# Layer 1's layer norm and transposes placed inside layer 0, the end of layer 0's last batch placed inside layer 1's scan

## The chip, the core and the metric

The kernel runs on one core of a Trainium2 chip. TensorE (PE) multiplies, VectorE (DVE), ScalarE (ACT) and GpSimd (POOL) do the element work, SyncE (SP) issues most DMAs. Every engine runs its own list of instructions strictly in the order in which the kernel writes it, and waits on semaphores for the others. The metric is device microseconds of one execution; the kernel before takes 2278.74 us (median of 3 runs, 2276.09 to 2279.93).

## The reference

Eight sequences (batches) of 512 tokens with 128 channels pass four layers; each layer is `xn = layernorm(x)`, then `x = x + attn(xn) + ffn(xn)`. The change concerns layers 0 and 1:

```python
# layer 0, attention: 16 heads of 8 channels with relative positions, then its own norm
ctx = softmax((q k^T + c2p + p2c) / scale) v
out = layernorm(ctx @ Wo + bo + xn, eps=1e-7) * ln_scale + ln_bias
# layer 0, ffn
ffn = xn @ sign(weight).T
# layer 1, attention: a minimal GRU in both directions, per channel, over the 512 tokens
z, h~ = sigmoid(xn @ Wz + bz), g(xn @ Wh + bh);  h[t] = (1 - z[t]) h[t-1] + z[t] h~[t]
out = concat(h_fwd, h_bwd) @ W_out + b_out
# layer 1, ffn: router xn @ w_router, the two best of 8 experts per token, 64 places per expert and
# sequence given out in order (a running count over tokens), experts with gelu, weighted sum back
```

Layers 2 (cross attention and a gated ffn) and 3 (channel attention and slots with 16 experts) are left as they were.

## The kernel before

X holds the tokens (32 tiles of 128 tokens by 128 channels, four tiles for a batch), XN the normed tokens and XT their transpose, all in SBUF. Each stage has one function per engine (`l0_pe`, `l0_dv`, ..., `l1_pe`, ...), and `after_l0` between them makes every engine wait for all of layer 0.

**Layer 0** is one pipeline of 512 steps, 64 for a batch: step u is one block of 128 queries of one head (16 heads times 4 blocks). In every step PE makes the scores, DVE adds the band (L181, form PS<-PS,AR) and takes the maximum (L193), ACT takes exp (L167) and copies the transposed probabilities (L171), POOL and the DMAs prepare the position terms two heads ahead. Small work of the neighbouring batches is put at fixed steps r of a batch, all of it through PSUM bank 7 (`B_M`), one use after another in the order of the list `order`. For the batch before these are `ENDS`: the last transposes of its heads (17), the transpose of the context (19), the output product `mo` (29), the ffn product `sw` (31), the square root on ACT (34), the norm on DVE (36, `tail(b, 2)`: a Newton step on 4 columns with `newton`, then four tensor_scalar of 128x128 by `ts`, L177), scale and sum on POOL (38), and statistics of the new X into NMV (48). The loop has 28 steps after the last (`STEPS0`), in which the last batch's end runs with nothing beside it. XN is in use there: it holds two of three buffers of the position terms (`CD`), the heads' output `OS` and the loaded scale, bias and output bias.

**Layer 1** begins with `after_l0`. Then SP issues 11 loads (L1082) and ACT two of 2 MB each (`wi`, `wo2`), and `norm_dv`, `norm_root`, `norm_po`, `norm_tr`, `norm_xt1` make XN and XT of all 32 tiles. PE then makes the 32 router products and starts the scan. The scan has 16 units, two directions for each batch. Unit u: two products of 128x512 on PE (`unit`), three sigmoids on ACT, `gate(u)` on DVE (L185), a multiplication on POOL, and on DVE the scan instruction of the unit before (`scan(u - 1)`, L1269). After the second unit of a batch PE makes the output products of the batch before (`scan_out`, 8 products of 128x128), and DVE adds them to X. DVE also runs the routing between units (`route(k)` after unit k: 0, 2, 3, 4 and 8); the running count over the tokens is 44 small products on PE (weights `trile` and `ones128`, 64 columns each), placed after unit 7. After the scan comes the dispatch: DVE builds one-hot tiles (DR), ACT and POOL split XN into a high and a low part (XH1 over XT, XL1), PE multiplies.

Of the kernel before, what the change touches and what calls it, by code (L numbers as in the profile page):

```python
# [13 lines left out]
SEQ = 512  # L14
# [204 lines left out]
def program(nc, a, out):  # L219
    ctx = ExitStack()  # L220
    with ctx:
# [13 lines left out]
        NMV = sb("NMV", [128, NT, 2])  # L235
        ar_at = -(-nc.sbuf_base // 32) * 32
        AR = sb("AR", [128, 40660])
# [133 lines left out]
        lst, lmv, ly, lv, ltmp = A0.take(4, 6), A0.take(4, 2), A0.take(4), A0.take(4), A0.take(4)  # L371
# [12 lines left out]
        ld_end = sem("ld_end")  # L384
# [10 lines left out]
        STEPS0 = 4 * NBH + 28  # L395
# [7 lines left out]
        ENDS = [{"heads": 17, "ct": 19, "mo": 29, "sw": 31, "root": 34, "norm": 36, "sum": 38, "last": 48}] * NB  # L403
        ENDS += [{"heads": 14, "ct": 16, "mo": 18, "sw": 19, "root": 21, "norm": 22, "sum": 23, "last": 25}]

        def small(u):
# [3 lines left out]
            if b >= 1 and r in (ENDS[b]["heads"], ENDS[b]["ct"], ENDS[b]["mo"], ENDS[b]["sw"]):  # L410
                uses += [(k, b - 1, 3 if k == "heads" else 0) for k in ("heads", "ct", "mo", "sw") if ENDS[b][k] == r]
# [6 lines left out]
        for u in range(STEPS0):  # L418
            order += small(u)
        number, emptied, n_ac, n_dv = {}, [], 0, 0  # L420
        for i, use in enumerate(order):
            number[use] = i
            if use[0] in ("q", "k", "far", "g0", "ct"):
# [13 lines left out]
        def l0_pe(pe):  # L437
# [13 lines left out]
            def small_mm(use):  # L451
# [124 lines left out]
            for u in range(STEPS0):  # L576
# [10 lines left out]
                if 0 <= G < 4 * NB and r in (0, 2, 4, 6):  # L587
                    pv(G, r // 2)


        def l0_dv(dv):
# [100 lines left out]
            def tail(b, k):  # L692
                ps, xs = quarters(PS[:, B_M, :]), slice(b * 4, b * 4 + 4)
                if k == 0:
                    dv.wait_ge(m_mm, number["mo", b, 0] + 1)
                    dv.wait_ge(ld_end, 3 * 16)
                    tt(dv, T1, ps, bc(bot.unsqueeze(1), [128, 4, 128]), ALU.add).then_inc(m_dv, 1)
                elif k == 1:
# [6 lines left out]
                    ts(dv, lv, lmv[:, :, 1], 1e-7, None, ALU.add).then_inc(tn_v, 1)  # L705
                elif k == 2:
                    dv.wait_ge(tn_v, b + 1)
                    dv.wait_ge(tn_q, b + 1)
                    dv.step(newton(dv, ly, lv, ltmp))
# [3 lines left out]
                    ins.then_inc(tn_n, 1)  # L713
                else:
# [7 lines left out]
            for u in range(STEPS0 + 1):  # L722
# [8 lines left out]
                if b >= 1:  # L731
                    at = ENDS[b]
                    if r == at["heads"] + 1:
                        heads_out(b - 1, 3)
                    if r == at["mo"] + 1:
                        tail(b - 1, 0)
                    if r == at["sw"] + 1:
                        tail(b - 1, 1)
                    if r == at["norm"]:
# [1833 lines left out]
```

## Time and profile before

| | us |
|---|---|
| median of 3 runs | 2278.74 (2276.09 to 2279.93) |
| the profiled execution's own time | 2277.15 |
| its span | 2275.3 |
| layer 0's products end | about 929 |
| last batch's end, on all engines | 929 to 945 |
| layer 1's norm and transposes | 945 to 962 |
| router products | 962 to 975 |
| scan with routing | 975 to 1047 |

Busy over the whole span: PE 85%, DVE 78%, ACT 63%, POOL 54%. That mean says little here: in layer 0 PE and DVE are near their limits together, while between 929 and 1047 us one engine after another waits for a chain. The profiled execution's own time is 1.85 us more than its span, and the median is 1.6 us more than the profiled execution.

### The profile page before, as it was taken

The numbers are of one execution on the slowest core, as the hardware profiler recorded it, in microseconds if no ns is written. First come the engines' busy times: TensorE is split into PE (matmuls) and PEld (weight loads), VectorE is DVE, ScalarE is ACT, GpSimd is POOL, SyncE is SP. The second block draws the span as 40 slices with busy tenths as digits, with TensorE's granted clock in tenths as the row PEclk, the third lists the DMA queues.
The fourth block names the chain that finished last, engine by engine and source line by source line (L and its number), as shares of the span: only waits on it lengthen the run. The fifth ranks groups of instructions, "written<-read, shape, count | busy, mean of one in ns | idle before, by whom it ended". The sixth has DMA issues, their size and how long they took to land.

```text
span 2275.3 us, 38965 instructions
## 1 busy us (share of the span) xinstructions
PE 1944.4 (85%) x13526; PEld 1473.7 (65%) x13526; DVE 1763.7 (78%) x4099; ACT 1430.5 (63%) x2795; POOL 1223.2 (54%) x1028
## 2 busy tenths in 40 slices
PE   3799898888989898587996999999998468788898
PEld 2566565666666666464683878777876345566797
DVE  7688888888888888457187888888887699873586
ACT  2578777777878777344235666666665257765575
POOL 3777677777777775148053445444543466426400
PEclk9999999999999999789997999999999689999999
DMA  3988788888878786201000000000001000003000
GB/s 105 306 304 303 249 294 274 288 268 278 284 271 281 278 300 227 85 1 35 3 6 1 1 1 1 1 1 1 1 1 31 0 0 1 1 1 98 24 2 38
DMA packets 73877, 264.15 MB, mean 116 GB/s; under 512 B 12273, under 2 KB 32241, under 8 KB 73169
## 3 DMA queue, kind: packets, MB, share of 16 engines
q1 hardware_dynamic: 72304, 254.31, 33.2%
q10 hardware_dynamic: 1376, 7.34, 0.8%
q8 instruction: 109, 1.79, 0.3%
q14 instruction: 88, 0.71, 0.1%
HBM read 140.30 MB, written 121.31 MB: 115 GB/s over the span
## 4 chain that ended last, share of the span: by engine, by line
PE 38%; DVE 8%; ACT 6%; POOL 2%; issue 2%; DMA 0%; POOLq 0%; ACTq 0%; DVEq 0%; SPq 0%
PE PS L157 10%; PE PS L161 7%; PE PS L163 7%; PE PS L162 7%; PE PS L326 7%; ACT AR L167 3%; ACT L167 2%; DVE AR L181 1%; DVE DR L181 1%; DVE PT L181 1%; ACT AR L171 1%; ACT PT L171 1%; DVE AR L185 1%; DVE AR L200 1%; DVE AR L193 1%
## 5 line engine op out<-in xcount | busy, mean ns | idle before, releaser
L167 ACT ACTIVATE AR<-PS,AR 128x512 f32<-128x512 f32 x1008 | 686.6, 688 | 286.8 <-DVE AR L193 178.8
L193 DVE TENSOR_REDUCE AR<-PS 128x1 f32<-128x512 f32 x896 | 616.4, 688 | 119.3 <-PE PS L163 100.5
L326 PE MATMUL PS<-ident,AR 128*128 128x128 f32 x3816 | 584.6, 277 | 86.1 <-ACT AR L171 38.6
L157 PE MATMUL PS<-AR 128*9 128x512 f32 (+8 forms) x4190 | 503.5, 360 | 93.0 <-DVE AR L181 32.9
L326 PEld LDWEIGHTS PS<-ident,AR 128*128 128x128 f32 x3816 | 435.0, 142 | 200.6 <-issue 71.2
L181 POOL TENSOR_TENSOR AR<-AR 128x512 f32<-128x512 f32 (+6 forms) x310 | 380.6, 1244 | 226.9 <-DVE AR L181 97.0
L157 PEld LDWEIGHTS PS<-AR 128*9 128x9 f32 (+5 forms) x4190 | 288.8, 133 | 298.4 <-DVE AR L181 130.1
L171 ACT ACTIVATE AR<-PS 128x512 f32<-128x512 f32 (+3 forms) x612 | 356.4, 587 | 91.8 <-PE PS L326 47.7
L176 POOL TENSOR_SCALAR AR<-AR 128x512 f32<-128x512 f32 x144 | 245.4, 1704 | 293.2 <-DVE AR L1596 219.4
L171 ACT ACTIVATE PT<-PS 128x512 fp32r<-128x512 f32 x320 | 191.5, 599 | 208.3 <-PE PS L326 171.5
L181 DVE TENSOR_TENSOR PS<-PS,AR 128x192 f32<-128x192 f32 (+1 forms) x512 | 201.7, 394 | 118.0 <-PE PS L534 112.0
L181 DVE TENSOR_TENSOR AR<-PS,AR 128x512 f32<-128x512 f32 (+3 forms) x321 | 210.0, 655 | 40.8 <-PE PS L157 36.2
L181 POOL TENSOR_TENSOR AR<-XN,AR 128x192 f32<-128x192 f32 (+1 forms) x170 | 201.5, 1206 | 60.9 <-DMA XN<-scr 42.9
L181 DVE TENSOR_TENSOR PT<-PS,PT 128x512 fp32r<-128x512 f32 x320 | 217.7, 680 | 5.0 <-ACT PT L171 5.0
L181 POOL TENSOR_TENSOR AR<-AR,XN 128x512 f32<-128x512 f32 x144 | 154.3, 1074 | 104.4 <-DVE AR L181 74.8
L534 PE MATMUL PS<-AR 128*128 128x320 bf16 (+3 forms) x1024 | 197.3, 275 | 0.0
L531 PE MATMUL PS<-ident,XN 128*128 128x128 f32 x680 | 131.1, 275 | 0.0
L161 PE MATMUL PS<-MH,XNr 128*128 128x512 f32 x256 | 123.5, 483 | 5.2 <-ACT AR L167 2.8
L176 DVE TENSOR_SCALAR AR<-AR 128x512 f32<-128x512 f32 (+6 forms) x229 | 113.9, 501 | 1.3
L534 PEld LDWEIGHTS PS<-AR 128*128 128x128 bf16 x1024 | 101.1, 99 | 6.2
L163 PE MATMUL PS<-MH,XNr 128*128 128x512 f32 x256 | 102.1, 399 | 0.0
L161 PE MATMUL PS<-PT,VW 128*128 128x512 f32 x256 | 101.5, 396 | 0.0
(157 smaller groups left out, 3001.9 us busy)
## 6 DMA issues: line engine op xcount, KB each, us to landing
scr<-AR SPq DMA_DIRECT2D x128, 800.0 KB, 4.3
XN<-scr SPq DMA_DIRECT2D x85, 768.0 KB, 6.6
AR<-scr SPq DMA_DIRECT2D x43, 768.0 KB, 6.5
AR<-qsc SPq DMA_DIRECT2D x96, 192.0 KB
qsc<-AR SPq DMA_DIRECT2D x96, 128.0 KB, 3.4
AR<-in_wgu SPq DMA_DIRECT2D x16, 256.0 KB, 3.2
X<-in_x ACTq DMA_DIRECT2D x1, 2048.0 KB, 8.5
AR<-in_wi ACTq DMA_DIRECT2D x1, 2048.0 KB, 8.2
```

The lines of the kernel that those rows point to most:

```text
L157: return pe.e.matmul(out, lhsT, rhs, start=start, stop=stop)
L161: pe.e.matmul(out, l[0], r[0], start=start, stop=False)
L162: pe.e.matmul(out, l[1], r[0], start=False, stop=False)
L163: return pe.e.matmul(out, l[0], r[1], start=False, stop=stop)
L167: return ac.e.activation(out, in_, func, bias=bias, scale=scale, accum_out=accum)
L171: return ac.e.activation(out, in_, ACT.Copy, bias=0.0, scale=1.0)
L176: return en.e.tensor_scalar(out, in0, s1, None, op0)
L181: return en.e.tensor_tensor(out, in0, in1, op)
L193: return dv.e.tensor_reduce(out, in_, AX.X, ALU.max, negate=True)
L326: return pe.e.transpose(out, in_, ident[0:k, 0:k])
L531: pe.e.matmul(out, lhsT, rhs, start=start, stop=start, is_transpose=True, skip_group_check=True)
L534: return pe.e.matmul(out, lhsT, rhs, start=False, stop=stop, skip_group_check=True)
```

## The change

**Layer 0.** In batches 2 to 7 of the pipeline, the norm at step 36 (`tail(b, 2)`, b from 1 to 6) also norms the tokens of batch b - 1 for layer 1. Its Newton step takes 8 columns instead of 4; a copy stores the scale in NY, and four more tensor_scalar of 128x128 write the normed tokens to XR, a buffer that otherwise holds the splits of q and k. At step 45 PE transposes XR (4 products) into bank 7, and at step 46 ACT copies them to XT. So the first six batches are transposed before layer 0 ends. `STEPS0` goes from 28 extra steps to 14, without the last batch's end.

**Layer 1.** Each engine begins the scan once `pv_mm` says that layer 0's last products are made. SP's 11 loads wait for that too; the two 2 MB loads come from SP now, after `after_l0`, and lie where nothing of layer 0 is needed. `END0` puts the last batch's end between the units of the scan: heads 0, ct 1, mo 2, sw 3, root 4, norm 5, sum and xt (batch 6's transposes) 6, last 7, and the last batch's own norm for layer 1 at root7 8, norm7 9, tr7 10. DVE writes the normed tokens of batch u into XN after unit u (`normed`, units 0 to 6). The router products are cut into eight groups of four (`ROUTER`). The routing moves to units 13, 14 and 15 with its last part after the scan, and the running count (`trail`) from after unit 7 to after unit 15's products. Exp and the normalization of the router's probabilities come after the scan.

VectorE at step 36 of a batch in layer 0, before (AR is the working area, T1 in it; the last row is the next batch's v with its bias):

```order
L208 RECIPROCAL AR<-AR 128x4 [waits l0_tn_q,l0_tn_v]
L181 TENSOR_TENSOR AR<-AR 128x4 [waits own_dv] x2
L177 TENSOR_SCALAR AR<-AR 128x4 [waits own_dv]
L181 TENSOR_TENSOR AR<-AR 128x4 [waits own_dv]
L177 TENSOR_SCALAR AR<-AR 128x128 [waits own_dv]
L177 TENSOR_SCALAR AR<-AR 128x128 x3
L181 TENSOR_TENSOR AR<-PS,AR 128x64x8 [waits l0_pv,l0_m_mm]
```

The same place of the changed kernel:

```order
L208 RECIPROCAL AR<-AR 128x8 [waits l0_tn_q,l0_tn_v]
L181 TENSOR_TENSOR AR<-AR 128x8 [waits own_dv] x2
L177 TENSOR_SCALAR AR<-AR 128x8 [waits own_dv]
L181 TENSOR_TENSOR AR<-AR 128x8 [waits own_dv]
L177 TENSOR_SCALAR AR<-AR 128x128 [waits own_dv]
L177 TENSOR_SCALAR AR<-AR 128x128 x3
L730 COPY NY<-AR 128x4 [waits l0_sp_a,l0_sp_p]
L177 TENSOR_SCALAR AR<-X,NMV,AR 128x128 x4
L181 TENSOR_TENSOR AR<-PS,AR 128x64x8 [waits l0_pv,l0_m_mm]
```

A copy and four tensor_scalar stand between the norm and what the pipeline does next.

VectorE in the scan, two units of the kernel before with nothing between them (L185 is a gate, L1269 a scan, the row with X the output of a batch):

```order
L185 SCALAR_TENSOR_TENSOR AR<-PS,AR 128x512 [waits l1_sig,l1_u_mm]
L1269 SCALAR_TENSOR_TENSOR AR<-AR 128x512 [waits l1_gz_po]
L185 SCALAR_TENSOR_TENSOR AR<-PS,AR 128x512 [waits l1_sig,l1_u_mm]
L1269 SCALAR_TENSOR_TENSOR AR<-AR 128x512 [waits l1_gz_po]
L181 TENSOR_TENSOR X<-X,PS 128x512 [waits l1_bout,l1_so_mm]
```

Unit 5 of the changed kernel (its scan is L1335):

```order
L185 SCALAR_TENSOR_TENSOR AR<-PS,AR 128x512 [waits l1_sig,l1_u_mm]
L1335 SCALAR_TENSOR_TENSOR AR<-AR 128x512 [waits l1_gz_po]
L181 TENSOR_TENSOR X<-X,PS 128x512 [waits l1_bout,l1_so_mm]
L177 TENSOR_SCALAR XN<-X,NMV,NY 128x128 x4
L208 RECIPROCAL AR<-AR 128x8 [waits l0_tn_q,l0_tn_v]
L181 TENSOR_TENSOR AR<-AR 128x8 [waits own_dv] x2
L177 TENSOR_SCALAR AR<-AR 128x8 [waits own_dv]
L181 TENSOR_TENSOR AR<-AR 128x8 [waits own_dv]
L177 TENSOR_SCALAR AR<-AR 128x128 [waits own_dv]
L177 TENSOR_SCALAR AR<-AR 128x128 x3
L730 COPY NY<-AR 128x4
L177 TENSOR_SCALAR AR<-X,NMV,AR 128x128 x4
```

Twelve tensor_scalar of 128x128 and a Newton step stand in one unit here; other units carry less.

TensorE at the end of the scan of the changed kernel, from unit 15's products on (`l1_rt_dv` is the routing's semaphore; 128x8x8 are the 64 columns of the running count, and DR the dispatch):

```order
L157 MATMUL PS<-XT,AR 128x512 [waits l1_sig]
L157 MATMUL PS<-XT,AR 128x512 [waits l1_g_dv]
L157 MATMUL PS<-AR 128x128 [waits l1_so_dv,l1_scan]
L157 MATMUL PS<-AR 128x128 x7
L157 MATMUL PS<-AR 128x8x8 [waits l1_ones,l1_rt_dv]
L157 MATMUL PS<-AR 128x8x8 x35
L157 MATMUL PS<-AR 128x128 [waits l1_so_dv,l1_scan]
L157 MATMUL PS<-AR 128x128 x7
```

The eight rows have the same forms as those after unit 7 before, where units 8 to 15 still follow; here the last output products and the dispatch follow.

The diff, cut to its core:

```diff
-        STEPS0 = 4 * NBH + 28
+        STEPS0 = 4 * NBH + 14
-        ENDS = [{"heads": 17, ..., "last": 48}] * NB
-        ENDS += [{"heads": 14, "ct": 16, "mo": 18, "sw": 19, "root": 21, "norm": 22, "sum": 23, "last": 25}]
+        ENDS = {"heads": 17, "ct": 19, "mo": 29, "sw": 31, "root": 34, "norm": 36, "sum": 38, "xt": 45, "last": 48}
+            if 2 <= b < NB and r == ENDS["xt"]:
+                uses.append(("xt", b - 2, 0))
...
+                elif what == "xt":
+                    pe.wait_ge(tn_n, 2 * b + 3)
+                    for q in range(4):
+                        ins = tr(pe, ps[:, q * 128:q * 128 + 128], XR[:, q * 128:q * 128 + 128])
...
+                    w = 8 if b else 4
+                    dv.step(newton(dv, ly[:, 0:w], lv[:, 0:w], ltmp[:, 0:w]))
...
+                    if b:
+                        done = 6 * min(b + 3, NB)
+                        dv.wait_ge(sp_p, done)
+                        dv.wait_ge(sp_a, done)
+                        dv.step(dv.e.tensor_copy(NY[:, 4 * b - 4:4 * b], ly[:, 4:8]))
+                        for i in range(4 * b - 4, 4 * b):
+                            ins = ts(dv, XR[:, i % 4 * 128:i % 4 * 128 + 128], X[:, i, :], NMV[:, i, 0:1], ly[:, 4 + i % 4:5 + i % 4],
+                                     ALU.subtract, ALU.mult)
+                        ins.then_inc(tn_n, 1)
...
+            def xt_out(b):
+                ac.wait_ge(m_mm, number["xt", b, 0] + 1)
+                copy(ac, XT[:, b * SEQ:b * SEQ + SEQ], PS[:, B_M, :]).then_inc(m_ac, 1)
...
+        END0 = {"heads": 0, "ct": 1, "mo": 2, "sw": 3, "root": 4, "norm": 5, "sum": 6, "xt": 6, "last": 7, "root7": 8, "norm7": 9,
+                "tr7": 10}
+        ROUTER = {1: (0, 4), 2: (4, 8), 3: (8, 12), 4: (12, 16), 5: (16, 20), 7: (20, 24), 9: (24, 28), 12: (28, 32)}
         def l1_sp(sp):
+            sp.wait_ge(pv_mm, 4 * NB)
...
+            after_l0(sp)
+            for dst, name in ((wi, "wi"), (wo2, "wo2")):
+                sp.e.dma_start(dst, a[name]).then_inc(ld[1], 16)
...
+            for u in range(16):
+                unit(u)
+                for what, b, g in (("heads", LAST, 3), ("ct", LAST, 0), ("mo", LAST, 0), ("sw", LAST, 0), ("xt", LAST - 1, 0)):
+                    if u == END0[what]:
+                        small_mm((what, b, g))
+                if u in ROUTER:
+                    for i in range(*ROUTER[u]):
+                        ins = mm(pe, PS[:, 6, i * 8:i * 8 + 8], XT[:, i * 128:i * 128 + 128], router, True, True)
...
+                if u % 2 and u >= 3:
+                    scan_out(u // 2 - 1)
+                if u == END0["tr7"]:
+                    pe.wait_ge(xn_dv, NB)
...
+            pe.wait_ge(m_ac, n_ac + 1)
+            trail()
             scan_out(NB - 1)
+            after_l0(pe)
...
+            ROUTE = {13: (0,), 14: (3,), 15: (4,)}
             for u in range(16):
                 gate(u)
                 if u:
                     scan(u - 1)
                 if u % 2 and u >= 3:
                     scan_out(u // 2 - 1)
-                route(u)
+                for k in ROUTE.get(u, ()):
+                    route(k)
+                if u < LAST:
+                    normed(u)
...
             scan(15)
+            route(8)
             scan_out(7)
+            after_l0(dv)
```

## Rows read from the trace of the kernel before

**Rows 1.** Busy time by stage: start:end, length, then each engine's (count), TensorE clock, DMA share, GB/s.

```profile
170.00:830.00 660.00, 588.64 (x5157) 418.95 (x5156) 560.73 (x1206) 505.12 (x894) 494.68 (x447) 1.00 0.83 280
928.80:945.40 16.60, 4.49 (x32) 3.67 (x32) 5.39 (x23) 2.68 (x4) 3.78 (x3) 0.76 0.00 0
945.40:961.80 16.40, 7.88 (x33) 6.33 (x33) 12.78 (x64) 5.19 (x12) 4.91 (x6) 0.50 0.76 291
961.80:975.40 13.60, 13.60 (x64) 13.60 (x65) 0.00 (x0) 0.00 (x0) 0.00 (x0) 0.50 0.00 0
975.40:1047.30 71.90, 56.84 (x265) 36.71 (x265) 50.08 (x62) 34.75 (x60) 46.01 (x31) 0.93 0.00 1
```

**Rows 2.** Timeline at the boundary: start, length, engine, line, form, count.

```profile
925.16 3.62 PE L157 MATMUL PS<-AR 128*9 128x512 f32 x32 [0.69 <-ACT AR L171]
1004.16 9.99 PE L157 MATMUL PS<-AR 128*128 128x64 f32 x88
1047.26 6.71 DVE L181 TENSOR_TENSOR DR<-AR 128x512 fp32r<-128x512 f32 x11
```

**Rows 3.** Chain of waits through one pair of units of the scan.

```profile
1025.77 2.93 PE PS L157 x18
1028.72 0.90 ACT AR L167 x2
1030.67 0.75 DVE AR L185
1031.42 1.14 DVE AR L1269
```

**Rows 4.** Timeline of ACT: when layer 0's output OS (in XN) is copied, every 16 steps.

```profile
119.66 0.60 ACT L171 ACTIVATE XN<-PS 128x512 f32<-128x512 f32 x1
143.83 0.60 ACT L171 ACTIVATE XN<-PS 128x512 f32<-128x512 f32 x1
435.20 0.60 ACT L171 ACTIVATE XN<-PS 128x512 f32<-128x512 f32 x1
467.38 0.60 ACT L171 ACTIVATE XN<-PS 128x512 f32<-128x512 f32 x1
```

**Rows 5.** Timeline of DVE and POOL at step 36 of a batch in layer 0.

```profile
450.84 2.36 POOL L181 TENSOR_TENSOR AR<-XN,AR 128x192 f32<-128x192 f32 x2 [0.58 <-DVE PS L181]
...
451.54 1.88 DVE L181 TENSOR_TENSOR AR<-AR 128x4 f32<-128x4 f32 x2
...
453.85 1.12 DVE L177 TENSOR_SCALAR AR<-AR 128x128 f32<-128x128 f32 x4
454.88 0.69 DVE L181 TENSOR_TENSOR AR<-PS,AR 128x512 f32<-128x512 f32 x1
```

**Rows 6.** Timeline of SP's queue: the first and the twelfth load at the kernel's start.

```profile
0.72 0.39 SPq L2479 DMA_DIRECT2D ident<-in_ident  x1
6.82 0.45 SPq L2484 DMA_DIRECT2D AR<-in_l_sw  x1
```

**Rows 7.** DMA issues by line at the start: count, KB, us to landing.

```profile
ident<-in_ident SPq DMA_DIRECT2D x1, 96.0 KB, 2.2
```

**Rows 8.** Timeline of ACT at the start of the scan.

```profile
977.57 1.28 ACT L167 ACT_TABLE_LOAD   x1 [15.95 <-PE PS L157]
978.87 3.58 ACT L167 ACTIVATE AR<-PS,AR 128x512 f32<-128x512 f32 x6
```

**Rows 9.** Timeline of DVE: the routing's second choice between two units.

```profile
998.70 1.43 DVE L185 SCALAR_TENSOR_TENSOR AR<-AR 128x256 f32<-128x256 f32 x1
1001.98 0.42 DVE L181 TENSOR_TENSOR AR<-AR 128x256 f32<-128x256 f32 x1
```

**Rows 10.** Busy time in stretches of 2 us around a fall and a rise of the clock.

```profile
986.00:988.00 2.00, 0.00 (x0) 0.00 (x0) 0.56 (x1) 2.00 (x5) 1.30 (x2) 1.00 0.00 0
988.00:990.00 2.00, 0.62 (x3) 0.63 (x4) 1.97 (x4) 1.07 (x2) 1.73 (x1) 0.65 0.00 0
994.00:996.00 2.00, 2.00 (x5) 0.77 (x4) 1.86 (x5) 1.10 (x2) 0.75 (x1) 0.64 0.00 0
```

More of the change, by code:

```diff
@@ L744, in l0_dv @@
                     heads_out(b, HEADS.index(r - 1))
-                if b >= 1 and r == ENDS[b]["last"]:
+                if 1 <= b < NB and r == ENDS["last"]:
                     tail(b - 1, 3)
+            return heads_out, tail
         def l0_ac(ac):
@@ L927, in l0_po @@
                     split(b + 1, k // 2, k % 2)
-                if b >= 1 and r == ENDS[b]["sum"]:
+                if 1 <= b < NB and r == ENDS["sum"]:
                     tail(b - 1)
+            return tail
         def l0_sp(sp):
@@ L1057, in program @@
         H_ = [A1.take(512) for _ in range(4)]
+        assert A1.top <= PTN * 2048
+        wi, wo2 = A1.take(8, 512), A1.take(8, 4, 128)
         XIN = A1.take(8, 8, 64)
@@ L1276, in scan_out, with normed @@
                 tt(dv, X[:, xs, :], X[:, xs, :], quarters(PS[:, 4 + b % 2, :]), ALU.add).then_inc(so_dv, 1)
+            def normed(b):
+                dv.settle()
+                for i in range(4 * b, 4 * b + 4):
+                    ins = ts(dv, XN[:, i, :], X[:, i, :], NMV[:, i, 0:1], NY[:, i:i + 1], ALU.subtract, ALU.mult)
+                ins.then_inc(xn_dv, 1)
+            ROUTE = {13: (0,), 14: (3,), 15: (4,)}
             for u in range(16):
@@ L1283, in l1_dv @@
                     scan_out(u // 2 - 1)
-                route(u)
+                for k in ROUTE.get(u, ()):
+                    route(k)
+                if u < LAST:
+                    normed(u)
+                if u == END0["heads"]:
+                    heads_out(LAST, 3)
+                if u == END0["mo"]:
+                    tail(LAST, 0)
+                if u == END0["sw"]:
+                    tail(LAST, 1)
+                if u == END0["norm"]:
+                    tail(LAST, 2)
+                if u == END0["last"]:
+                    tail(LAST, 3)
+                    dv.settle()
+                    ts(dv, v7, NMV[:, 4 * LAST:NT, 1], 1e-5, None, ALU.add).then_inc(tn_v, 1)
+                if u == END0["norm7"]:
+                    dv.wait_ge(tn_v, NB + 1)
+                    dv.wait_ge(tn_q, NB + 1)
+                    dv.step(newton(dv, NY[:, 4 * LAST:NT], v7, tmp7))
+                    dv.settle()
+                    normed(LAST)
             scan(15)
+            route(8)
             scan_out(7)
+            after_l0(dv)
             dv.wait_ge(rt_dv, 3)
@@ L1293, in l1_dv @@
                    ALU.is_equal).then_inc(d_dv, 1)
+            dv.wait_ge(a_ac, 49)
+            dv.step(red(dv, s8, PROB, ALU.add))
+            dv.settle()
+            dv.step(dv.e.reciprocal(s8, s8))
+            dv.settle()
+            tt(dv, PROB, PROB, col(s8), ALU.mult).then_inc(rt_dv, 1)
             for p in range(4):
@@ L2485, in run_sp @@
             l0_sp(sp)
-            after_l0(sp)
             l1_sp(sp)
```

234 lines of the change are left out of this document (123 added, 111 removed).

## The prediction

> **What bounds the kernel now.** I read the page first: TensorE 85%, VectorE 78%, and a low stretch in slices 16 to 18. The busy time by stage says what that is [rows 1]. In layer 0, 660 us of its middle hold 588.6 us of PE and 560.7 us of DVE work, 89% and 85%: two engines near their limit that also wait for each other. From 928.8 us on nothing is near a limit: 16.6 us for the last batch's end (DVE 5.4 us busy, PE 4.5), 16.4 us for layer 1's norm, 13.6 us in which only PE works, at a granted clock of 0.50, and 71.9 us of scan with DVE at 50.1 us. Then I read the timeline at the boundary [rows 2]: layer 0's last products end at 925.16 + 3.62 = 928.8 and the dispatch begins at 1047.3 with DVE's first DR tile. These 118.5 us are what the change rewrites. Last the chain of waits in the scan [rows 3]: output products and the next unit's first product 2.93, two sigmoids 0.90, a third one until 1030.67, gate 0.75, scan 1.14, and again; a pair of units takes 1032.6 - 1025.8 = 6.8 us, and DVE is free for about 1.3 us of it.
>
> **Layer 0, what is added.** Six times, at step 36, DVE gets a copy, a small tensor_scalar and four tensor_scalar of 128x128. Four of these take 454.88 - 453.85 = 1.03 us to the next instruction [rows 5]; for the two small ones I add 0.3, which makes 1.35 us. At step 45 PE gets four transposes, about 0.5, and ACT a copy of 0.6 like those of rows 4. Is it hidden? The same place tells: the 16 steps after step 28 take 143.83 - 119.66 = 24.2 us in batch 0, which has no batch before it, and 467.38 - 435.20 = 32.2 us in batch 3, which has the products, statistics, square root and norm of the batch before [rows 4]. So 8.0 us are paid for some 6 us of DVE work, 3 of PE and 3 of ACT: nothing of DVE's part is hidden, and a bit more than DVE's part is paid, since PE and DVE wait for each other in turn. For the new work I take 2.2 us a batch: 1.35 of DVE, 0.5 of PE, and 0.35 for bank 7, which is now used at 45 and again at 47. Six batches: +13.2 us. The lower end is DVE's alone with a fifth of it absorbed, 1.1 us a batch or 6.6; a gain is excluded, since nothing is taken from these steps. The upper end takes the ratio 8.0 to 6 on all of it with the whole bank handover, 3.0 a batch or 18.
>
> **Layer 1, from the end of layer 0's products (0) to the first DR tile.** Removed: the 16.6 us of the last batch's end, the 16.4 of the norm and the 13.6 of the router as stretches of their own.
>
> *Start.* SP's 11 loads are issued only at 0. Twelve went out from 0.72 to 6.82, 0.55 apart, and the first landed 2.2 after its issue [rows 6, 7]: ten distances and a landing are 7.7 us. PE is idle for them, and the clock will be low, since an idle PE from before 986 to 989 lost it by 990 [rows 10]. A product of 0.90 then takes 1.8, then table load 1.28, three sigmoids 1.8 (six took 3.58 [rows 8]): first gate at 12.6. Before, the tail of layer 0 ran in this time; now nothing does.
>
> *The scan is now DVE's.* Its 50.1 us stay, without 1.3 for the probabilities that move behind the dispatch's start. Added: the last batch's end 5.4 [rows 1], eight batches normed into XN at 1.03 with a small wait, 8.8, batch 6's XR and copy 1.2, statistics of the last batch 1.3, its Newton step 1.2. That makes 66.7, of which 4.0 (last scan, last part of the routing, last output) come after the running count: 62.7. To it come DVE's remaining waits, for which I walked through the units in the order of the code with these durations: 1.7 in units 0 and 1 (chain as in rows 3); 1.5 for the first output products behind `mo`, `sw` and router products on PE; 0.8 at unit 4 for the square root between two table loads; 3.0 at unit 7, because PE's transposes of batch 6 wait for DVE's norm at unit 5 and unit 7's products stand behind them; 2.2 at unit 9 for the second square root's table loads; 1.5 at unit 11 behind the last batch's transposes; 2.8 in the bare pairs 10 to 13. Together 13.5. The second choice of the routing ends at 12.6 + 62.7 + 13.5 = 88.8.
>
> The router's products, 64 records of 0.21 at half clock in 13.6 us, are some 0.9 a group at full clock and fall into time in which PE waits for DVE: 0. The 2 MB loads need no one before the expert products: 0. The probabilities' sum, reciprocal and product stand on DVE where it waits for expert products: 0; POOL's first weights, now behind them, have that slack too.
>
> *The running count.* 88 records took 9.99 us at full clock in the middle of PE work [rows 2]. Now they stand behind unit 15, and DVE makes the second choice just before: a gate, a scan, an output and 1001.98 + 0.42 - 998.70 = 3.7 us of choice [rows 9], while PE has only one batch's output products (2.0). PE is idle for some 6 us, longer than before the fall at 988 to 990 [rows 10]. At 0.50 the count begins at 0.21 us a record as the router's did. The clock came back by 995 after some 5 us of output products and unit products [rows 10], and did not come back in 13.6 us of router products [rows 1]. The count has 64 columns where these have 128, 512 and 8. I take a rise after 5 us: 23 records in 5 us, 65 in 7.4, 12.4 in all. Ends: 10.0 and 19.
>
> *End.* After the count output products 2.0 and DVE's addition 0.7: first DR at 88.8 + 12.4 + 2.7 = 103.9 instead of 118.5, that is -14.6.
>
> **Sum.** -14.6 + 13.2 = -1.4. The profiled execution took 2277.15 (span 2275.3, 1.85 around it), so 2275.8; the median lies 1.6 above it: 2277.4, rounded to 2277.5.
>
> The Trainium skill bears on two terms. POOL's two band products occupy 450.84 to 453.2, and DVE's two products on 4 columns, begun at 451.54, take 1.88 us [rows 5]: they end when POOL does. "SBUF — State Buffer" (engine ports, the shared port pair) calls it an exclusive lock between a GpSimd operation and a DVE operation with two SBUF inputs or in a two-port mode. By it the moved choice would be slowed by POOL's multiplications, as 3.7 us for five short instructions already shows, and the tensor_scalar only in a two-port mode; with 0.5 us for half of the 48 new ones the sum would be some 12 us worse, an estimate, and a rival below has that mechanism. "ScalarE: Activation LUTs" (What ACT_TABLE_LOAD costs) gives 1.28 us and a drain of 1.38 for each switch. The trace agrees with the first and shows 0.02 us from the load's end to the next sigmoid [rows 8]. By the page four added loads would be 5.5 us dearer, by the rows nothing.
>
> **The rivals.**
> - *Layer 0 hides half* (faster). DVE has 15% free and PE 11% in the mean [rows 1]; if the pipeline catches up behind step 36, layer 0 costs 6.6 instead of 13.2, and with a count at full clock (-2.4): -10.4, so 2268.5. Against it: 8.0 us paid for the same kind of work [rows 4].
> - *The count at half clock* (slower). The place is behind unit 15. If 64 columns count as little as the router's 8, 88 records take 19 and the output products behind them 2 more: +8.6, total +7.2, 2286. It decides once DVE's work keeps PE idle so long that the clock falls before the count and the count does not raise it again; with a clock that stays, the count costs 10.
> - *DVE held by POOL* (slower). In the scan DVE's load no longer leaves the 1.3 us a pair in which collisions vanished. If half of the 16 scans and 32 tensor_scalar lose 0.5 us each, that is +12: 2289. For it: 1.88 us for two products of 4 columns [rows 5]; against it: four tensor_scalar took no more than 1.12.
>
> **How the numbers follow.** This kernel's measurement can tell about 0.2%, 4.6 us, from no change. The forecast, a change between -4.6 and +4.6, has 0.38; the hidden half and its milder forms 0.33; the count at half clock 0.19; POOL's lock, or full cost in layer 0 with a half-clock count, 0.10. Faster 0.33, same 0.38, slower 0.29. Layer 0 leaves -6.6 to +5, the count -2.4 to +8.6, the scan's waits 4 either way; they seldom fall together, so 2265 to 2290 holds 8 in 10. The likeliest case's own range is 2273 to 2283.
>
> **What would show it.** In the changed profile: the distance of OS copies from step 28 to 44 should be 34 to 35 us in batches 2 to 7 (32.2 before), and layer 0's products should end at 939 to 945. First gate 12 to 13 us after them. DVE busy at least 0.7 of the scan. Running count 88 records in 12 to 19 us, with a clock near 0.5 at its start; first DR some 104 us after layer 0's products. The prediction is wrong if OS copies stay at 32.2, if PE does not lose its clock before the count, or if the stretch takes more than 112 us.

## The result

The changed kernel takes 2286.44 us (median of 7 runs, 2283.89 to 2288.79) against 2278.74 for the kernel before (median of 7 runs in the same session, 2276.09 to 2284.00): ratio 1.0032, 95% interval 1.0020 to 1.0043. The same kernel measured again, in 11 runs, gave 2286.78 and 1.0030 (1.0020 to 1.0040); its profile is called the second one below. The forecast was 2277.5, a change of -1.4; it is slower by 7 to 8 us. The profiled execution took 2286.73 with a span of 2284.9.

Where it went is read at the boundary of layers 0 and 1. First the timeline of PE and DVE in the changed kernel, answering [rows 2]: start, length, engine, line, operation, form, count, and in brackets the idle time before and what ended it.

```profile
940.89 3.62 PE L157 MATMUL PS<-AR 128*9 128x512 f32 x32 [0.69 <-ACT AR L171]
951.05 3.78 PE L157 MATMUL PS<-XT,AR 128*128 128x512 f32 x4 [6.53 <-DMA AR<-in_rev]
1035.26 19.14 PE L157 MATMUL PS<-AR 128*128 128x64 f32 x88 [6.80 <-DVE AR L181]
...
956.49 0.75 DVE L185 SCALAR_TENSOR_TENSOR AR<-PS,AR 128x512 f32<-128x512 f32 x1 [5.13 <-PE PS L157]
...
1055.04 6.71 DVE L181 TENSOR_TENSOR DR<-AR 128x512 fp32r<-128x512 f32 x11
```

Layer 0's products end at 940.89 + 3.62 = 944.5, 15.7 us later than before. The first gate follows 12.0 us behind, and the running count begins 90.75 us behind. It has 72 of the 88 records, two for each of its 36 products; the other 16 records are the last 8 output products, and the 44 products given for the count in the section on the kernel before are both together. The dispatch begins 1055.04 - 944.51 = 110.5 us behind layer 0's products, where it was 118.5. So: +15.7 in layer 0, -8.0 in layer 1. In the second profile layer 0's products end at 942.0 and the dispatch begins 111.0 us behind them: +13.2 and -7.4. From the first DR tile to the end of the span it is 1228.0 us before, 1229.9 after and 1228.1 in the second profile: behind the boundary no change is clear of what profiles of one kernel differ by.

Second, busy time of the three stages of layer 1, answering [rows 1]: start:end, length, each engine's busy time (count), granted TensorE clock, DMA share, GB/s.

```profile
944.50:956.50 12.00, 5.47 (x14) 2.74 (x12) 0.34 (x5) 3.77 (x6) 0.20 (x1) 0.72 0.18 47
956.50:1035.30 78.80, 54.22 (x271) 36.05 (x269) 68.33 (x127) 38.33 (x64) 48.69 (x31) 0.93 0.13 54
1035.30:1055.00 19.70, 19.10 (x88) 18.80 (x88) 3.33 (x6) 0.00 (x0) 2.78 (x5) 0.52 0.00 0
```

The last row is the news: 19.7 us in which PE does nearly all the work, at half clock. In steps of 4 us around it (same columns):

```profile
1028.00:1032.00 4.00, 0.46 (x5) 0.26 (x3) 3.93 (x7) 1.28 (x7) 2.19 (x2) 1.00 0.00 2
1032.00:1036.00 4.00, 0.74 (x4) 0.75 (x4) 3.83 (x7) 0.00 (x0) 4.00 (x6) 0.72 0.00 0
1036.00:1040.00 4.00, 4.00 (x20) 4.00 (x20) 0.60 (x1) 0.00 (x0) 2.08 (x4) 0.50 0.00 0
...
1048.00:1052.00 4.00, 4.00 (x20) 4.00 (x20) 1.05 (x3) 0.00 (x0) 0.00 (x0) 0.50 0.00 0
1052.00:1056.00 4.00, 2.42 (x13) 2.16 (x11) 1.99 (x5) 0.00 (x0) 0.00 (x0) 0.72 0.00 0
```

PE is nearly idle from 1028 to 1035, the clock falls from 2.4 to 1.2 GHz in the second row, and it stays at 0.50 through some 16 us of unbroken work of 64-column products. It is back only in the last row, near the end of the output products (128 columns), which begin at about 1051.

Layer 0 shows as forecast in the copies of OS on ACT [rows 4]:

```profile
435.68 0.60 ACT L171 ACTIVATE XN<-PS 128x512 f32<-128x512 f32 x1
469.06 0.60 ACT L171 ACTIVATE XN<-PS 128x512 f32<-128x512 f32 x1
```

33.4 us in this batch (34.6 in the second profile), 35.0 and 34.3 in the two behind it, against 32.2 before; the 16 steps behind, which hold the new transposes, take 25.5 instead of 24.7.

### The profile page after: what moved, and what is told of

Same layout as the page of the kernel before. It is cut to its first block, busy times and chain, and to the rows that moved or that the text cites. A ratio compares the mean times of both kernels' runs of the same rounds, so it can differ in the third digit from the quotient of the medians.

```text
span 2284.9 us, 39010 instructions
## 1 busy us (share of the span) xinstructions
PE 1947.4 (85%) x13526; PEld 1478.5 (65%) x13526; DVE 1776.3 (78%) x4127; ACT 1431.9 (63%) x2794; POOL 1222.8 (54%) x1024
## 3 DMA queue, kind: packets, MB, share of 16 engines
q10 hardware_dynamic: 1088, 3.15, 0.4%
## 4 chain that ended last, share of the span: by engine, by line
PE 61%; DVE 20%; ACT 9%; issue 5%; POOL 3%; DMA 2%; SPq 0%; POOLq 0%; ACTq 0%; DVEq 0%
PE PS L157 19%; PE PS L326 14%; PE PS L161 7%; PE PS L163 7%; PE PS L162 7%; DVE AR L181 4%; ACT AR L167 4%; DVE AR L193 3%; PE PS L541 3%; PE PS L538 3%; ACT AR L171 2%; POOL AR L181 2%; DVE XN L177 2%; ACT L167 2%; DVE PS L181 2%
## 5 line engine op out<-in xcount | busy, mean ns | idle before, releaser
L157 PE MATMUL PS<-AR 128*9 128x512 f32 (+8 forms) x4190 | 514.7, 365 | 97.3 <-DVE AR L181 47.7
L326 PEld LDWEIGHTS PS<-ident,AR 128*128 128x128 f32 x3844 | 440.7, 142 | 206.3 <-issue 82.5
L157 PEld LDWEIGHTS PS<-AR 128*9 128x9 f32 (+5 forms) x4190 | 298.2, 136 | 301.5 <-DVE AR L181 146.1
L162 PE MATMUL PS<-MH,XL 128*128 128x512 f32 x256 | 102.2, 399 | 0.0
```

The costliest lines, as they stand in the source:

```text
L157: return pe.e.matmul(out, lhsT, rhs, start=start, stop=stop)
L162: pe.e.matmul(out, l[1], r[0], start=False, stop=False)
L326: return pe.e.transpose(out, in_, ident[0:k, 0:k])
```

## The experiments

**What makes the count slow.** Theory A: PE stands idle for DVE's second choice, the clock falls, and the narrow count cannot raise it. First, the idle time was filled with work that nothing needs.

```diff
             pe.wait_ge(m_ac, n_ac + 1)
+            pe.wait_ge(ld[1], NL1 + 32)
+            for k in range(7):
+                mm(pe, PS[:, 7, :], w1[k % 4], wi[:, k, :], True, True)
             trail()
```

> The changed kernel with seven 128x512 products on weights already loaded put in front of the running count, into the bank that the count then overwrites; PE thus works through the 6.8 us in which it waited for the second choice. Theory A (the count is slow because PE stood idle before it and the clock fell to 0.50): granted clock 1.00 in the count, the group of 88 records takes 10 us instead of 19.1, first DR tile about 9 us earlier, total 2277 to 2279. Rival B (the group is slow for its waits or for its 64-column products whatever stood before): the clock is 0.50 again or the group stays at 17 to 19 us, total 2285 to 2288. Rival C (the count is faster but something else releases the dispatch): group at 10 us, first DR less than 4 us earlier, total above 2282.

Measured: 2275.44 us (12 runs), ratio to before 0.9988 (0.9980 to 0.9996). The group in the timeline of its profile, and the clock while it ran:

```profile
1034.38 10.09 PE L157 MATMUL PS<-AR 128*128 128x64 f32 x88 [0.80 <-DVE AR L181]
```

```profile
1036.00:1040.00 4.00, 4.00 (x38) 4.00 (x38) 0.00 (x0) 0.00 (x0) 1.21 (x3) 1.00 0.00 0
```

The same 88 records take 10.09 us at 2.4 GHz instead of 19.14 at 1.2; the dispatch begins 103.4 us behind layer 0's products instead of 110.5. Theory A stands: useless work of 6 us makes the kernel 11 us faster by the medians, 10 by the ratios to the kernel before. 7 to 8 us of them are seen at this place. Single profiles can't be held to the microsecond: in seven profiles of kernels with the same layer 0 its products end between 939.4 and 946.0.

**Is it the idle alone, or the narrow products too?** The same filling with 28 products of 64 columns:

```diff
-            for k in range(7):
-                mm(pe, PS[:, 7, :], w1[k % 4], wi[:, k, :], True, True)
+            for k in range(28):
+                mm(pe, PS[:, 7, 0:64], w1[k % 4], wi[:, k % 8, 0:64], True, True)
```

> The changed kernel with 28 products of 64 columns in front of the running count in place of the seven of 512 columns of the filled kernel; at full clock they take about as long (28 x 0.22 = 6.2 us). Theory A1 (what keeps TensorE's clock is that it works at all): clock 1.00 in the count, 88 records in 10 us, total 2275 to 2278 as with wide filling. Theory A2 (narrow products do not hold or raise the clock, as the 72 records of the count and the router's did not raise it): clock 0.50 in the count, filling itself slower (up to 12 us), 88 records in 19 us, total 2286 to 2293. In both the records of the filling alone tell it.

Measured: 2284.73 us, ratio 1.0039 (1.0025 to 1.0053). Its count, and its PE in stretches around the count's start:

```profile
1036.62 16.60 PE L157 MATMUL PS<-AR 128*128 128x64 f32 x88 [0.62 <-DVE AR L181]
```

```profile
1032.00:1036.00 4.00, 3.99 (x36) 3.85 (x35) 3.86 (x7) 0.00 (x0) 4.00 (x5) 1.00 0.01 2
1036.00:1040.00 4.00, 3.38 (x24) 3.39 (x25) 1.92 (x3) 0.00 (x0) 3.45 (x6) 0.82 0.01 4
1038.00:1039.00 1.00, 1.00 (x10) 1.00 (x9) 0.00 (x0) 0.00 (x0) 1.00 (x4) 0.80 0.06 16
1040.00:1044.00 4.00, 4.00 (x21) 4.00 (x21) 0.00 (x0) 0.00 (x0) 0.00 (x0) 0.50 0.00 0
```

The filling itself ran at full clock, which A2 had not said, and so did the first 2 us of the count. Then the clock fell, at 1038 to 1039, in a stretch in which PE was busy all the time. So neither theory holds as it was written: in these runs the narrow products did not bring the clock back (some 16 us in the changed kernel, 13.6 in the router before), and here they did not keep it either. The 9.99 us of the count in the kernel before passed at 1.00 with 128x512 products right ahead of it, as in the kernel with the wide filling.

**Does the late place do it by itself?** The kernel before, with nothing but its routing steps moved to units 14 and 15 and the count behind unit 15:

```diff
-                if b == 3:
+                if b == 7:
+                    scan_out(b - 1)
                     pe.wait_ge(rt_dv, 2)
...
-                route(u)
+                route({3: 1, 4: 1, 8: 1, 14: 3, 15: 4}.get(u, u))
             scan(15)
+            route(8)
             scan_out(7)
```

> The kernel before with nothing but its first and second choice moved from units 3 and 4 to units 14 and 15 of the scan and the running count from behind unit 7 to behind unit 15 and the output products of batch 6. Theory A (the late place alone brings the idle and the half clock): PE waits some 6 us for the second choice, the group of 88 records takes 18 to 19 us at a granted clock of 0.50; against before the stretch loses the whole group of 10 us from the scan's middle only where PE was the limit there, so total 9 to 15 us above before, 2288 to 2294. Rival (the half clock comes from the changed kernel's own scan, in which PE idles for DVE's added work): the clock stays at 1.00 and the total is 3 to 6 us above before.

Measured: 2291.25 us, ratio 1.0056 (1.0038 to 1.0073), that is +11.6.

```profile
1044.50 19.14 PE L157 MATMUL PS<-AR 128*128 128x64 f32 x88 [6.41 <-DVE AR L181]
```

The same 19.14 us, with 6.41 of idle ahead. The clock in the count was 0.50 here too. The loss needs nothing of the changed kernel's DVE load; it belongs to the place.

**Choice one unit earlier.**

```diff
-        ROUTER = {1: (0, 4), 2: (4, 8), 3: (8, 12), 4: (12, 16), 5: (16, 20), 7: (20, 24), 9: (24, 28), 12: (28, 32)}
+        ROUTER = {1: (0, 4), 2: (4, 8), 3: (8, 12), 4: (12, 16), 5: (16, 20), 7: (20, 24), 9: (24, 28), 11: (28, 32)}
...
-            ROUTE = {13: (0,), 14: (3,), 15: (4,)}
+            ROUTE = {12: (0,), 13: (3,), 14: (4,)}
```

> The changed kernel with the last router group at unit 11 instead of 12 and the three routing steps on DVE at units 12, 13, 14 instead of 13, 14, 15: when PE is through with unit 15 the second choice should be there. Theory A: the count begins without a long idle at a clock of 1.00, takes 10 us, and lies beside DVE's gate 15, scans and output addition; 9 us for the clock and up to 4 for the overlap, less what PE waits for at unit 11 (the copy of the last tokens): first DR 8 to 12 us earlier, total 2274 to 2279. Rival B (small-column products are slow by themselves): the count still takes 15 us, gain only from the overlap, 3 to 4 us, total 2282 to 2284. Rival D (the last tokens arrive too late at unit 11, PE waits there and the clock falls there): no gain, 2285 to 2289.

Measured: 2280.84 us, with single runs from 2271.15 to 2286.86; ratio 1.0001 (0.9986 to 1.0017). Inconclusive as a median; its profile, of a run of 2284.44, shows one way in which it fails:

```profile
1030.14 2.84 PE L157 MATMUL PS<-AR 128*128 128x128 f32 x16 [3.15 <-DVE AR L1335]
1033.78 18.62 PE L157 MATMUL PS<-AR 128*128 128x64 f32 x88 [0.80 <-DVE AR L181]
```

```profile
1024.00:1028.00 4.00, 2.99 (x7) 0.97 (x6) 3.86 (x7) 3.54 (x6) 3.09 (x2) 1.00 0.00 0
1028.00:1032.00 4.00, 1.86 (x13) 1.86 (x14) 3.93 (x6) 3.33 (x11) 2.12 (x1) 0.90 0.00 0
1032.00:1036.00 4.00, 3.20 (x16) 2.90 (x15) 3.90 (x7) 0.00 (x0) 1.54 (x1) 0.50 0.01 2
```

The wait right before the count is gone (0.80), but 3.15 us of idle one group earlier cost the clock as well, and the narrow count kept it low. With the clock kept it should be some 9 us less, and the runs at 2271 to 2273 would fit that. It is not shown: no profile of such a run was taken, and the kernel before spreads as widely, over 9.7 to 16.1 us in the four sets of its runs beside the experiments.

**The count in wider products.** 12 products of 64 to 256 columns instead of 36 of 64; the idle before stays.

```diff
-                    for q in range(4):
-                        prev = [(v, j) for j in range(q)] + ([(v1, j) for j in range(4)] if k else [])
-                        ins = mm(pe, ov[:, :, q, :], trile, v[:, :, q, :], True, not prev)
-                        for x, (pv_, j) in enumerate(prev):
-                            ins = mm(pe, ov[:, :, q, :], ones128, pv_[:, :, j, :], False, x == len(prev) - 1)
+                    mm(pe, ov, trile, v, True, False)
+                    prev = [(v, j, j + 1) for j in range(3)] + ([(v1, j, 0) for j in range(4)] if k else [])
+                    for x, (pv_, j, q0) in enumerate(prev):
+                        ins = mm(pe, ov[:, :, q0:4, :], ones128, bc(pv_[:, :, j:j + 1, :], [128, 8, 4 - q0, 8]), False, x == len(prev) - 1)
```

> The changed kernel with the same count written in 12 products of 64 to 256 columns instead of 36 of 64 columns (a product with the triangle over all four tiles of a batch, the earlier tiles' ones repeated in the moving operand); the 6.8 us idle before it stay. The columns stay 2304. By 0.45 us a record of 512 columns at full clock and 0.9 at half: 4.1 us at full, 8.1 at half, against 7.9 and 15.3 of the narrow form. Theory A3 (wider products raise the clock again): some 5 to 6 us and the output products behind at full clock, first DR 11 to 12 us earlier, total 2274 to 2276. Theory A4 (half clock throughout): 8.1 + 3.8 us, first DR 7 us earlier, total 2279 to 2280.

Measured: 2273.67 us, ratio 0.9987 (0.9977 to 0.9998).

```profile
1034.26 8.55 PE L157 MATMUL PS<-AR 128*128 128x256 f32 x40 [6.80 <-DVE AR L181]
```

```profile
1036.00:1038.00 2.00, 2.00 (x9) 1.82 (x8) 0.00 (x0) 0.00 (x0) 1.08 (x3) 0.50 0.00 0
1038.00:1040.00 2.00, 2.00 (x11) 1.90 (x10) 0.00 (x0) 0.00 (x0) 0.00 (x0) 0.72 0.00 0
1040.00:1042.00 2.00, 2.00 (x16) 1.90 (x15) 0.91 (x3) 0.00 (x0) 0.00 (x0) 1.00 0.00 0
```

Theory A3: after the same 6.80 us of idle the clock is back some 5 us into the group, as the forecast had it, only with wide products; 8.55 us in place of 19.14 for the count and the output products. The wide form has a third of the products for the same 2304 columns. Whether their width or their number matters to the clock, these runs do not separate.

**Layer 0's additions.** All of them left out for batches 0 to 5 (layer 1 then works on stale tokens), and only the transposes and copies left out (cut; the second change of the diff is in the first kernel alone, and in both the waits of other engines for what is gone are moved):

```diff
-            if 2 <= b < NB and r == ENDS["xt"]:
-                uses.append(("xt", b - 2, 0))
...
-                    if b:
+                    if b and b < NB - 1:
+                        dv.step(dv.e.tensor_copy(NY[:, 4 * b - 4:4 * b], ly[:, 4:8]))
+                    elif b:
```

> The changed kernel without what it adds to layer 0's pipeline in batches 0 to 5: the four 128x128 tensor_scalar at step 36, the four transposes and the copy at step 45. Layer 1 then works on stale tokens there; the reciprocal roots, the root with twice the width and layer 1's own order stay. Theory A (the additions cost 3.2 us a batch): layer 0's products end 19 us earlier, near 925, total 2267 +- 2. Rival E (2.2 us a batch as forecast, the rest of the later end comes from something else): 13 us, total 2273 +- 2. Rival F (only DVE's part counts): 8 us, total 2278.

> As the kernel without layer 0's additions, but with the four tensor_scalar a batch back in; left out are the transposes on PE and the copies on ACT for batches 0 to 5 (layer 1 works on stale tokens there). Theory A (DVE's part is paid in full and PE's and ACT's too): 6 x 1.35 = 8 us above the kernel without any, 11 us below the changed kernel: about 2275. Rival F (only DVE's part counts): equal to the changed kernel, 2286. Rival G (DVE has slack and only bank 7's handover counts): equal to the kernel without any, 2267.

Measured: 2272.24 us without any (ratio to before 0.9970, 0.9959 to 0.9981), 2281.38 with the tensor_scalar alone (1.0005, 0.9997 to 1.0014). From the changed kernel's 2286.4 to 2286.8 that makes 14.2 to 14.5 us for the whole, 9.1 for the tensor_scalar, 5.1 to 5.4 for the rest. The ends of layer 0's products, first without any, then with the tensor_scalar:

```profile
923.86 3.62 PE L157 MATMUL PS<-AR 128*9 128x512 f32 x32 [0.69 <-ACT AR L171]
```

```profile
931.27 3.62 PE L157 MATMUL PS<-AR 128*9 128x512 f32 x32 [0.69 <-ACT AR L171]
```

These ends, 927.5 and 934.9, are 17.0 and 9.6 us ahead of the changed kernel's 944.5, or 14.5 and 7.1 ahead of the second profile's 942.0. So the whole is 14 to 17 us, and the split is less certain than the medians make it look: 7.4 for the tensor_scalar by these two rows. The medians are lower because both kernels lose some 3 us again in layer 1. Their scan, from first gate to count, takes 82.2 us where it takes 78.8 and 79.6 in the changed kernel, at the same DVE work but a lower clock (row of the kernel without any); why the clock falls earlier there is open.

```profile
939.50:1021.70 82.20, 57.55 (x269) 38.81 (x268) 68.32 (x127) 38.27 (x64) 48.66 (x31) 0.88 0.13 52
```

In batch 3 the 32 steps from step 28 take 57.1 us without any, 58.1 with the tensor_scalar, 58.9 and 60.1 in the two profiles of the changed kernel: 1.9 to 3.0 us a batch where the forecast had 2.2. My expectation of 19 us for the whole (2267 in all) was too high, and the second kernel's 2281.38 lies between its theory A (2275) and rival F (2286); rival E (13 us, 2273) held, and the forecast's 13.2 (8.1 + 5.1) was nearly right.

**The norm in the scan.** Three of four tensor_scalar left out in seven batches (stale tokens in the dispatch):

```diff
-                for i in range(4 * b, 4 * b + 4):
+                for i in range(4 * b, 4 * b + 4 if b == LAST else 4 * b + 1):
```

> The changed kernel with three of the four tensor_scalar left out that write each of the first seven batches' normed tokens into XN in the scan (the dispatch then gets stale tokens for these). Step of the forecast: 8.8 us for eight batches at 1.03 each with a small wait. If DVE is the limit all through the scan and POOL's multiplications do not hold these instructions up: 7 x 0.77 = 5.4 us less. Theory P (they wait for POOL, as 2.0 to 5.1 us for a batch in the profile instead of 1.1 say): 8 to 12 us less where the held-up time goes with them. Rival (the held-up time only moves to the next DVE instruction, or PE and ACT take over as the limit): 3 to 5 us less. Total 2274 to 2283 in all, first gate to count 78.9 us in the changed kernel as it is.

Measured: 2279.65 us, ratio 1.0001 (0.9989 to 1.0013), 7 us less. Its scan from first gate to count:

```profile
951.30:1028.40 77.10, 56.36 (x271) 38.19 (x269) 58.49 (x106) 38.27 (x64) 48.63 (x31) 0.89 0.14 55
```

and the waits of DVE in that stretch, first of the changed kernel, then of this one (what waited, for what, us in total, times, longest):

```profile
DVE AR L185 <- ACT AR L167: 7.4, 4, 2.6
```

```profile
DVE AR L185 <- ACT AR L167: 19.9, 11, 5.1
```

DVE loses 9.8 us of work for 21 instructions, 0.47 each where a free one takes 0.28 [rows 5], and the stretch loses 1.7 (78.8 to 77.1; 2.5 against the changed kernel's second profile): the gates then wait for the sigmoids. The second row above also holds the first gate's wait of 5.1, which lies ahead of the stretch and which the first row lacks; without it the gates wait 14.8 us instead of 7.4, 7.4 more. The scan is not DVE's alone; PE, ACT, DVE and POOL take turns in it, and most of the work taken away was replaced by waits. How much of that is the clock's doing is open: PE's clock in the stretch was 0.89 here, 0.93 and 0.90 in the two profiles of the changed kernel. The medians differ by 7 us, more than the scan shows. In this profile layer 0, where nothing was edited, ends 2.5 to 5.1 us earlier than in the two of the changed kernel; where the rest of the 7 us lies stays open. The changed kernel, run once more to see whether its first median had been an accident:

> The changed kernel once more, unedited, beside the kernel before. The run without three quarters of the scan's norm work took 7 us less than the changed kernel by the medians, but its profile shows the scan only 1.7 us shorter and the rest of the difference in layer 0, where nothing was edited. If the changed kernel's first figure was right: 2285 to 2288 again, ratio 1.003. If part of the 7 us is how layer 0 happened to run: 2281 to 2284, ratio 1.001 to 1.002.

Measured: 2286.78 us, ratio 1.0030 (1.0020 to 1.0040). It had not.

**Loads earlier.** Layer 1's weights placed in buffers of layer 0's probabilities that are free one group of heads earlier:

```diff
-            sp.wait_ge(pv_mm, 4 * NB)
+            sp.wait_ge(pv_mm, 4 * NB - 1)
+        A1.top = 2 * 2048
         w1 = [A1.take(128) for _ in names1]
...
+        w1_end, A1.top = A1.top, 0
```

> The changed kernel with layer 1's weights and constants put where probabilities of layer 0 lie that are free one group of heads earlier, so that their 11 loads go out some 25 us before layer 0's products end. Expected: PE's wait of 6.5 us for the last load goes; first unit's products start 1 us after layer 0's products instead of 6.5, at full clock (0.9 us a product instead of 1.8): first gate 5 us after layer 0's products instead of 12.0, total 7 us less, 2279 to 2280. Rival (DVE or the head's end becomes the wait: the last head's reciprocal and product come first): first gate 8 to 9, total 2282 to 2283.

Measured: 2278.22 us, ratio 0.9999 (0.9983 to 1.0015): 8.2 to 8.6 less than the changed kernel. PE's next product follows without a wait, and DVE's first gate comes 4.4 us behind layer 0's products (939.72 + 3.62) instead of 12.0:

```profile
943.27 1.99 PE L157 MATMUL PS<-XT,AR 128*128 128x512 f32 x4
...
947.77 0.75 DVE L185 SCALAR_TENSOR_TENSOR AR<-PS,AR 128x512 f32<-128x512 f32 x1 [3.96 <-ACT AR L167]
```

Of these 7.6 us 5.9 to 6.5 reach the dispatch, which begins 104.6 us behind layer 0's products; the scan takes 80.8 us here, at a clock of 0.86.

**All together.** Early choice, wide count, early loads, with and without three wide products of filling at unit 15:

> The changed kernel with the choice one unit earlier, the wide count, the early loads and three 128x512 products as filling before the output products of unit 15. If the three gains add up (7 for the loads, 10 for the clock, up to 4 for the count beside DVE's last scans and 3.8 for the wide count): total 2262 to 2266, 13 to 17 us below the kernel before. If the count hides wholly behind DVE's gate 15, scans and output addition, the last terms overlap and it is 2265 to 2269. Rival (clock falls once in a while in the last units): single runs 4 us above.

> The kernel with the choice one unit earlier, the wide count and the early loads, without the three products of filling. If the clock falls behind unit 15's products in some runs, as it did with the early choice alone: the wide count takes 8 us instead of 4.4 and the dispatch begins about 3 us later; median 2266 to 2268 with runs at 2270, against 2264.75. If the clock stays without the filling: the same 2264 to 2266.

Measured: 2264.75 us with the filling (ratio 0.9955, 0.9939 to 0.9970), 2263.90 without (0.9934, 0.9920 to 0.9949). Both beat both kernels, and their intervals overlap, so no gain of the filling is shown. In the profile of the one without, PE and DVE from the output products of batch 6 on, and the clock at the count's start:

```profile
1022.48 3.16 PE L157 MATMUL PS<-AR 128*128 128x128 f32 x16 [3.13 <-DVE AR L1339]
1026.11 4.63 PE L157 MATMUL PS<-AR 128*128 128x256 f32 x24 [0.47 <-DVE AR L181]
1031.27 2.05 PE L157 MATMUL PS<-AR 128*128 128x128 f32 x16 [0.53 <-DVE AR L1339]
...
1033.96 4.84 DVE L181 TENSOR_TENSOR DR<-AR 128x512 fp32r<-128x512 f32 x7
```

```profile
1024.00:1026.00 2.00, 1.64 (x8) 1.34 (x7) 1.86 (x6) 0.00 (x0) 0.00 (x0) 0.50 0.00 0
1026.00:1028.00 2.00, 1.89 (x10) 1.79 (x11) 2.00 (x4) 0.00 (x0) 1.21 (x1) 0.85 0.00 0
1028.00:1030.00 2.00, 2.00 (x14) 1.84 (x13) 1.48 (x2) 0.00 (x0) 2.00 (x2) 1.00 0.01 4
```

The clock did fall behind the idle of 3.13, as with the early choice alone, but with the wide count it was back within the count's first 2 us. The count takes 4.63 us beside DVE's last scans, and the dispatch begins 90.3 us behind layer 0's products instead of 110.5.

## Why the prediction was wrong

The forecast was -14.6 in layer 1 and +13.2 in layer 0, -1.4 in all; measured were -7.4 to -8.0 in layer 1's stretch, +13.2 to +15.7 in layer 0 and +7.1 to +7.7 in all, by the medians.

- *The running count: the step that failed.* "I take a rise after 5 us: 23 records in 5 us, 65 in 7.4, 12.4 in all." From the first record to the first DR tile I had 12.4 + 2.7 = 15.1 us; it took 19.78, which is 4.7 of the some 9 us by which the forecast was too low. The fall before the count was forecast rightly (6 us of idle, measured 6.80). The rise was taken from [rows 10], where products of 128 and 512 columns run, though [rows 1] show 13.6 us of 8-column products at 0.50 and the prediction names that row. By [rows 10] (0.64 for 994 to 996) the clock is back at about 995.4 there, some 6 us after PE began again, not 5. With the wide filling the clock does not fall ahead of the count, and the group takes 10.09 us. After the fall the return hangs on the form: the same 2304 columns in 12 products had the clock back after some 5 us, in 36 products of 64 it stayed away. The rival "the count at half clock", 2286 with a chance of 0.19, is the mechanism that happened. That its 2286 meets the measured 2286.4 is luck: it had +8.6 for the count's place, where 4.7 more than forecast was measured, and the rest came from the scan and layer 0.
- *An error in the sum that hid part of it.* The 88 records of [rows 2] already hold the 16 of the output products, which the "End" step added again with 2.0. Without that the forecast for this place would have been 13.1, and the miss 6.7 instead of 4.7. The rival's "88 records take 19 and the output products behind them 2 more" counts them twice as well.
- *The scan.* Forecast were 62.7 of DVE work and 13.5 of waits, 76.2 in all; measured 78.8 (79.6 in the second profile), of which DVE was busy 68.3. The total was good, its reading was not: the tensor_scalar took longer beside POOL's multiplications, for which the prediction had nothing but "a small wait", and DVE's waits were 78.8 - 68.3 = 10.5 us, not 13.5. It also had no term for the clock inside the scan, which falls twice there (0.50 at 988 to 992, 0.74 at 1008 to 1012). In the changed kernel's timeline of DVE, once with POOL idle and once not:

```profile
973.24 1.11 DVE L177 TENSOR_SCALAR XN<-X,NMV,NY 128x128 f32<-128x128 f32 x4
...
989.76 5.14 DVE L177 TENSOR_SCALAR XN<-X,NMV,NY 128x128 f32<-128x128 f32 x4
```

  and of POOL at the second time:

```profile
988.79 2.11 POOL L181 TENSOR_TENSOR AR<-AR 128x512 f32<-128x512 f32 x1 [4.51 <-DVE AR L185]
990.86 2.61 POOL L181 TENSOR_TENSOR AR<-AR,XN 128x512 f32<-128x512 f32 x2
```

  Four of them took 5.14 us where free ones take 1.11 here and 1.12 in [rows 5]; in the seven batches four take 1.99 to 5.14 beside POOL's work and 1.11 where POOL is idle, 17.7 us together instead of 7.8. The Trainium skill, "SBUF — State Buffer" (Who interferes with whom), has DVE and GpSimd exclude each other while DVE runs in a two-port mode, which tensor_scalar can enter. The trace agrees as far as these durations go; whether these instructions ran in such a mode no run shows. The rival "DVE held by POOL" had a mechanism that the rows bear out, but not its price of 12 us: the 9.9 us by which these are longer are in the 68.3 us of DVE work, and the stretch came out 2.6 over the forecast. No run changed POOL's work, so POOL as the cause is read from the rows and not tested.
- *The start.* 12.6 forecast, 12.0 measured; taking away the loads' wait gives back 7.6 of it.
- *Layer 0.* 8.1 + 5.1 = 13.2 forecast; 9.1 + 5.1 to 5.4 by the medians of the two kernels that leave parts out, 14.5 to 17.0 by the ends of layer 0's products. The sign of [rows 4], 34 to 35, was met but for 33.4 in batch 3; part of the cost falls in the next 16 steps (25.5 instead of 24.7).
- *The balance.* -1.4 forecast. 4.7 more for the count, 2.6 for the scan, -0.6 for the start make about -8.0 for layer 1's stretch; with the 14.2 to 14.5 us that layer 0's additions cost by the medians that is +6.2 to +6.5, and +7.1 to +7.7 was measured. The remaining microsecond is not assigned, and the sum is no closer than that: the 14.2 to 14.5 have some 3 us of a slower scan taken off.
- *The signs.* None of the three that would have said "wrong" came true: the OS copies moved, PE lost its clock before the count, and the stretch took 110.5 us, not more than 112. They watched the fall of the clock and not its return, on which the sum hung; of the other signs, the group of 19.14 us against "12 to 19" and the first DR tile at 110.5 us against "some 104" point at it.

## What to carry to other kernels

Before a block of narrow products is moved, look at what stands ahead of it on PE: behind wide products it ran at full clock (9.99 and 10.09 us), behind an idle PE at half clock nearly to its end, with PE busy all the time (19.14). Write such a block wide (here 36 products of 64 columns became 12, and with the output products behind them 19.1 us became 8.6) or place it where wide products surround it. And when a stretch is called one engine's, count what that engine waits for once its work is taken away; here 9.8 us less of DVE work made the scan 1.7 to 2.5 us shorter.

## What the runs showed of the hardware

- Products of 64 columns, PE busy 4.00 of 4.00 us, left the granted clock at 0.50 through the whole count, some 16 us in the changed kernel and the same in the kernel before with the late count. Begun at full clock, such products ran at 1.00 through the narrow filling and the count's first 2 us, and then the clock fell to 1.2 GHz with PE still busy (0.80 at 1038 to 1039, 0.50 behind). The Trainium skill, "TensorE: Matmul & The Clock Gate" (What's actually happening), says that the gate follows how busy PE has been. The runs agree for the fall, behind 6.80 us of idle. For the return they show what that sentence does not tell: stretches in which the profile has PE busy for 4.00 of 4.00 us and the clock stayed at 0.50.
- The same scan took 78.8, 79.6 and 79.4 us in three profiles with the same instructions up to the count (changed kernel twice, wide count), and 82.2 and 82.1 in the two kernels that leave out work of layer 0; PE's clock in it was 0.93, 0.90, 0.90, 0.88 and 0.88.
- The fp32 tensor_scalar of 128x128 took 1.11 us for four with POOL idle and 1.99 to 5.14 us beside its multiplications.
- The count alone at full clock: 24 records of the wide form in 4.40 us (in the kernel with all three changes and the filling) against 72 of the narrow one in 7.9 (9.99 of [rows 2] less 2.05 for the output products), for the same 2304 columns.
